# An attention kernel's order by hand: the transpose of the row maxima in front of the first value products, and both runs of these and the values' transpose one unit later

## What is computed

```python
x = hidden_states                       # 16 batches x 512 rows x 256
xn = layernorm(x)
q, k = low_rank_proj(xn, q_a, q_b), low_rank_proj(xn, k_a, k_b)   # 16 heads of 16
v = xn @ v_w.T + v_b
att = softmax(causal(q @ k.T / 4))      # 512 x 512 for each head and batch
y = (att @ v) @ o_w.T + o_b
ffn = experts_choose_tokens(xn)         # 8 experts, 128 rows each per batch, silu between w1 and w2
out = x + y + ffn
```

## Time and profile before

| what | value |
|---|---|
| median of 3 runs | 1292.59 us (1291.87 to 1296.5) |
| profiled execution | 1295.71 us, its span 1293.8 us |
| granted TensorE clock, mean | 0.969 of full |
| TensorE (PE) busy | 1184.1 us, 92% |
| weight loads (PEld) | 819.8 us, 63% |
| VectorE (DVE) | 967.2 us, 75% |
| ACT | 668.7 us, 52% |
| POOL | 692.0 us, 53% |

### The profile page before, as it was taken

The page is one execution under the profiler, slowest core; times in us unless marked ns, Lnnn a source line. Parts: engine busy times, 40 slices in busy tenths (PEclk is TensorE's granted clock), DMA queues, the critical chain, the costliest instruction groups (busy, mean ns, idle before and its releaser), DMA issues. The chain is left out here.

```text
span 1293.8 us, 29459 instructions
## 1 busy us (share of the span) xinstructions
PE 1184.1 (92%) x8502; PEld 819.8 (63%) x8502; DVE 967.2 (75%) x3293; ACT 668.7 (52%) x1312; POOL 692.0 (53%) x1021
## 2 busy tenths in 40 slices
PE   6799999999999999999999998769999999999995
PEld 5545555555555555555555553348988888888885
DVE  3588888879889888888888879935666666666662
ACT  2357667667667677677667665522332323233320
POOL 1235344355355355345345443344888888888885
PEclk9779999999999999999999999979999999999998
DMA  5443443443443443443444342132555555556454
GB/s 141 114 116 83 116 116 100 116 116 98 115 115 98 115 115 99 115 115 100 113 115 112 100 99 67 34 114 38 111 99 95 114 93 102 94 100 109 85 78 53
DMA packets 106287, 130.31 MB, mean 101 GB/s; under 512 B 21580, under 2 KB 75476, under 8 KB 106196
## 3 DMA queue, kind: packets, MB, share of 16 engines
q1 hardware_dynamic: 76356, 94.46, 28.1%
q0 software_dynamic: 24576, 33.57, 15.6%
q10 hardware_dynamic: 5264, 1.32, 0.5%
HBM read 44.84 MB, written 33.55 MB: 61 GB/s over the span
## 5 line engine op out<-in xcount | busy, mean ns | idle before, releaser
L719 DVE CUSTOM_DVE_ANT_0 junk<-bank,rowmask 128x256 bf16<-128x256 f32 (+3 forms) x1024 | 454.9, 485 | 60.3 <-PE bank L866 38.0
L565 ACT ACTIVATE probs<-bank 128x512 f32<-128x512 f32 x640 | 377.3, 598 | 158.0 <-PE bank L887 143.8
L469 POOL TENSOR_SCALAR_AFFINE_SELECT probs<-probs 128x256 f32<-128x256 f32 (+1 forms) x640 | 224.2, 363 | 311.0 <-ACT probs L565 308.9
L866 PE MATMUL bank<-kstk,qstk 96*128 96x256 bf16 (+3 forms) x1024 | 250.7, 306 | 34.3 <-DVE rowmax L719 17.3
L887 PE MATMUL bank<-qstk,kstk 98*128 98x256 bf16 (+3 forms) x1024 | 251.0, 307 | 3.8 <-ACT probs L565 2.6
L1049 POOL DMA_INDIRECT out_rows<-mixed,rows x128 | 208.9, 1632 | 58.2 <-issue 38.1
L1078 ACT ACTIVATE hid<-bank 128x512 f32<-128x512 f32 x128 | 76.6, 598 | 228.5 <-PE bank L1141 228.5
L908 PE MATMUL bank<-probs,vaug 128*32 128x512 f32 (+3 forms) x2048 | 168.5, 448 | 6.6 <-POOL probs L469 6.6
L1157 PE MATMUL bank<-w_hi,hid_hi 128*128 128x256 f32 x512 | 147.3, 288 | 0.0
L1157 PE MATMUL bank<-w_hi,hid_lo 128*128 128x256 f32 x512 | 144.9, 283 | 0.0
L1157 PE MATMUL bank<-w_lo,hid_hi 128*128 128x256 f32 x512 | 144.8, 283 | 0.0
(11 more groups left out here) (131 smaller groups left out, 2097.8 us busy)
## 6 DMA issues: line engine op xcount, KB each, us to landing
qstk<-qk_part SPq DMA_DIRECT2D x96, 256.0 KB, 4.8
kstk<-qk_part SPq DMA_DIRECT2D x96, 256.0 KB, 4.7
xln<-in_L_attn_hidden_states SPq DMA_DIRECT2D x16, 512.0 KB, 6.1
xn_rows<-xn SPq DMA_DIRECT2D x16, 512.0 KB, 2.8
xres<-in_L_attn_hidden_states SPq DMA_DIRECT2D x16, 512.0 KB, 3.6
out_rows<-xres SPq DMA_DIRECT2D x16, 512.0 KB, 2.9
qstk<-in_L_ffn_w SPq DMA_DIRECT2D x8, 512.0 KB, 4.0
kstk<-in_L_ffn_w SPq DMA_DIRECT2D x8, 512.0 KB, 3.9
```

The source lines that it names most:

```text
L469: nc.gpsimd.affine_select(out=block, in_=block, compare_op=ALU.is_ge, fill=0.0, base=0, pattern=[[0, len(cols)], [1, P]], channel_multipli ...
L565: nc.scalar.activation(probs[n % 2][:, 512 * k:512 * k + 512], SCORET[k % 2][:], ACT.Exp, scale=SCALE).then_inc(exp_done, 1)
L719: last = nc.vector.tensor_tensor_reduce(out=junk[k % 2][:, col:col + width], in0=SCORE[score_bank(UN * n + k)][:, col:col + width], in1=ro ...
L866: last = nc.tensor.matmul(SCORE[score_bank(UN * n + k)][:, col:col + width], qstk[b % 2][0:KS, GH * g + h, P * i:P * i + P], kstk[b % 2][0 ...
```

## The change

In all four kinds of slot maxt stays in unit 3 but is now ahead of value blocks 0 and 1, which move from unit 2 to unit 3. Value blocks 2 and 3 move from unit 5 to unit 6, ytr from unit 7 to unit 8. maxd stays in unit 4. The prologue, `PROJECTIONS` and the routing steps are as they were.

```diff
@@ -47,10 +47,10 @@
      (8, "qk_first", 2, 3), (9, "qk", 2, 3)])
 
 SUMS = (
-    [(2, "pv", 0, 0), (2, "pv", 0, 1), (3, "maxt", 2, 0), (4, "maxd", 2, 0), (5, "pv", 0, 2), (5, "pv", 0, 3), (7, "ytr", 0, 0)],
-    [(2, "pv", 0, 0), (2, "pv", 0, 1), (3, "maxt", 2, 0), (4, "maxd", 2, 0), (5, "pv", 0, 2), (5, "pv", 0, 3), (7, "ytr", 0, 0)],
-    [(2, "pv", 0, 0), (2, "pv", 0, 1), (3, "maxt", 2, 0), (4, "maxd", 2, 0), (5, "pv", 0, 2), (5, "pv", 0, 3), (7, "ytr", 0, 0)],
-    [(2, "pv", 0, 0), (2, "pv", 0, 1), (3, "maxt", 2, 0), (4, "maxd", 2, 0), (5, "pv", 0, 2), (5, "pv", 0, 3), (7, "ytr", 0, 0)])
+    [(3, "maxt", 2, 0), (3, "pv", 0, 0), (3, "pv", 0, 1), (4, "maxd", 2, 0), (6, "pv", 0, 2), (6, "pv", 0, 3), (8, "ytr", 0, 0)],
+    [(3, "maxt", 2, 0), (3, "pv", 0, 0), (3, "pv", 0, 1), (4, "maxd", 2, 0), (6, "pv", 0, 2), (6, "pv", 0, 3), (8, "ytr", 0, 0)],
+    [(3, "maxt", 2, 0), (3, "pv", 0, 0), (3, "pv", 0, 1), (4, "maxd", 2, 0), (6, "pv", 0, 2), (6, "pv", 0, 3), (8, "ytr", 0, 0)],
+    [(3, "maxt", 2, 0), (3, "pv", 0, 0), (3, "pv", 0, 1), (4, "maxd", 2, 0), (6, "pv", 0, 2), (6, "pv", 0, 3), (8, "ytr", 0, 0)])
 
 
 def slot_steps(b, g):
```

## The result

The changed kernel takes 1341.7 us (median of 4 runs, 1338.5 to 1344.7) against 1294.6 us for the kernel before in the same session: ratio 1.0357, 95% interval [1.0317, 1.0396]. That is 47 us slower, twice the 24 us that were forecast; the direction was right, the size was not.

What follows compares the result with a forecast made beforehand. TensorE was taken to bound the attention part. Kind 3 10.0, kind 2 7.5, kind 0 7.3 and the last slots -0.7 summed to +24.1 us on 1292.6: about 1316 us, forecast 1308 to 1323, range 1299 to 1324.

Steps and rivals of the forecast that it cites:

- Kind 3: Unit 3: TensorE waits 0.99 us for ACT's exponential 1; +0.82 us in fourteen slots, less 1.5 us of POOL waits: 10.0 us.
- Kind 2 up to the values: Score 3 moves from 444.92 to 445.46, held by VectorE; the transpose waits for xt_lo; values begin at 446.15.
- Kind 0, odd blocks: Loss of +0.8 us, filled in by the 1.51 us wait for the DMAs stacking q and k: 0.
- Kind 0 at the turn: Loop's even blocks: some 2 us idle ahead of score 3, and 0.6 us ahead of unit 9's v step by ytok.
- Cases 1 to 3: Rivals: drain alone, 1282 us, chance 0.08; part of the loss, 1305 us, 0.17; no change to tell, 1286 to 1299, 0.10.
- case 4: Rival: xres chain on POOL holds kind 3's masks, each block loses a further 1 us: 1330 us, chance 0.05.
- Kind 2 ... +0.67: Values 2 and 3 plus unit 6 end later: +0.67 us in odd blocks, +0.4 in even, seven each: 7.5 us.
- Kind 0, even blocks ... +1.51: Unit 9's v step waits for ytok's bank: +1.51 us, 0.15 comes back; 5 x 1.36 plus 0.5 for block 0: 7.3 us.
- The last eight slots ... I take -0.7 ... bounds -3 and +3: Slots with VectorE's ranking, taken as bound by VectorE: -0.7 us for a few saved hand-overs, bounds -3 and +3.
- The hand-over: Score, transpose, values together on TensorE: gain 0.17 us a slot, bounds 0.09 and 0.26; 11 us over 64 slots.
- By that rule alone the change wins: First rival, the drain alone: unit 3 of every slot, -11 us, 1282 us, waits absorbed; chance 0.08.

Runs made afterwards that it cites:

- The first half of the change by itself: Kernel before with the transpose and, behind it, value blocks 0 and 1 in unit 3; blocks 2, 3 and ytr unmoved: 1321.7 us, ratio 1.0221.
- filled: Changed kernel with unit 3's transposed score computed ten times in kind 0 of even blocks 2 to 12: 1334.5 us, ratio 1.0299.
- last_old: Changed kernel with the old order in the last eight slots: 1335.8 us, ratio 1.0313.
- ytr_in_7: Changed kernel with ytr alone back in unit 7: 1327.2 us, ratio 1.0252.
- maxt_behind_u2: Kernel before with only the maxima transpose moved, from unit 3 to unit 2 behind value blocks 0 and 1: ratio 1.0005 over 12 runs.
- second_late: Kernel before with only value blocks 2 and 3 moved to unit 6 and ytr to unit 8: 1315.3 us, ratio 1.0146.

## Why the prediction was right and wrong

**What held.** The moved value products cover nothing any more ahead of unit 3's waits, and the sign, the places and the releasers in kinds 3 and 0 were the ones named. Kind 3: 0.96 us of wait against 0.99, 0.75 us a slot against 0.82, 8.9 us in all against 10.0. Kind 2 up to the values: xt_lo's wait is there (3.9 us in 14 waits), and score 3 starts 0.26 us late (465.23) where I had 0.54. Kind 0, odd blocks: 0.04 us longer with kind 1, against 0. Kind 0 at the turn: v waits for ytok. The first half of the change by itself was expected at 26 us once the changed kernel's trace was known, and measured at 26, with its parts off by up to 3 us. Cases 1 to 3, all of which let the waits be absorbed in part or whole, are out, and so is case 4: POOL's wait vanished. The recorded text gives the forecast as 1308 to 1323 us in one place and 1299 to 1324 in another; 1341.7 us lies above both.

**What failed**, in the prediction's own steps:

1. *"Kind 2 ... +0.67"* and the sum of 7.5 us. Kind 2 is 1.29 to 1.35 us longer, 18.2 us in fourteen slots, of which kind 1 gives some back (0.4 us in even blocks). The missed term is the bank of ytr: I followed it into kind 0, where unit 9's v takes it, and not into kind 2, where unit 9's qk_first does by the same rule of two banks. It costs 0.44 us, 14 times, 6 us. Behind it the wait of the first xt, 0.3 us, was taken as covered and was so only in part: counted from the slot's first product, values 2 and 3 begin at 7.58 us where my walk has 7.40. In even blocks the discount I took was about right: 0.40 + 0.44 = 0.84 us for kinds 1 and 2 against a measured 1.29 - 0.36 = 0.93.
2. *"Kind 0, even blocks ... +1.51"*. Measured 2.8 us. The waits were there as sized, and behind the long one the clock fell. I had read a granted clock of 1.00 in the kernel before and taken durations from it, without asking what an idle stretch three times as long may do to it; the sum has no term for the clock. A fall costs 1.4 us, by `filled` and within `last_old`, and in the profiled execution all five turns had one: 7 us. That it was five and not three or none is in part luck.
3. *"The last eight slots ... I take -0.7 ... bounds -3 and +3"*. Measured +7.2 us in the profiled execution, and 4 to 7 by the other traces. I argued that VectorE bounds these slots (it is busy for 80.7 of 92.8 us there, TensorE for 74.7), and did not walk one of them. The bounds were too narrow for a part that no row was read from.

Together 6 + 7 + 8 = 21 us. The two profiled executions lie 49 us apart, so 25 are missing from the 24. By place: kinds 0 to 2 of the even blocks 21.7 us for 10.1, of the odd blocks 10.5 for 4.7, kind 3 8.9 for 10.0, block 14 and behind 7.2 for -0.7, ahead of the slots 0.8 for 0. The first xt's wait accounts for a part of the 4 us that the three steps leave; the rest is not traced. All three have one sign: each was something that I had not followed to its end, and a late step finds only waits there.

**The hand-over.** I took 0.17 us a slot; the values start 0.01 us behind the transpose (478.15 to 478.16), so that the gain there is at the upper bound, 0.25 us; where the transpose itself had waited the values follow later, 0.13 us in kind 2 (465.91 to 466.04) and 0.08 at the turn in `ytr_in_7` (386.58 to 386.66). And it is worth nothing in time, as `maxt_behind_u2` shows. The Trainium skill, TensorEngine Tiling (Array Packing), Key Properties, has the drain only where the tiling mode changes. The trace agrees with both halves of it, 0.09 us where the mode changes and 0.01 us between two steps where it stays and neither waits. By that rule alone the change wins; the rule says nothing of what the moved products had been covering.

## What to carry to other kernels

In an order written by hand, long products on the bounding engine are also the time in which the others catch up. Before moving such a block past a wait, list what each engine finishes during it, and walk every kind of slot, also the ones at the loop's turn and at the end. A step that frees a shared buffer later has to be followed to the next user of that buffer in each kind; and where TensorE gets new idle stretches, of 2 us or of less than 1, the sum needs a term for the clock, with bounds (here 0 to 1.4 us a turn).

## What the runs showed of the hardware

- After an idle stretch of 2.0 us on TensorE the granted clock fell from 1.00 to 0.5, and 1.64 us of value products took 3.05 us; with the stretch filled they took 1.64 us. With the same steps and the same 2.0 us the clock fell in 3 of 5 turns of `last_old`, in another order (`ytr_in_7`) in none, and in `second_late` in 3 of 5, with waits ahead of score 3 of at most 0.8 us. The runs do not settle what decides.
- VectorE stands still for 2.97 us at the turn of the loop, with no releaser in the trace, and for 2.63 us at the same turn of the changed kernel. Only the even blocks have it; their kind 0 is 1.6 us longer than the odd blocks' before and 3.8 us after, 1.4 of these 3.8 being the fallen clock.
- Steps that use a tile of 32 columns follow each other after 0.01 us, or 0.08 to 0.13 us in slots where TensorE had just waited, while the entry from a full-width product costs 0.09 us.
